# A graph layer on one core: the order of the work is set by a table of quarters, the taken edges run three quarters apart from iteration 36 on, extra tiles come every seven quarters, and two tiles are left behind the last sum

## The reference, cut to what matters

```
def reference(x, src, dst, edge_type_3, node_type_3, W_e, b_e, W_n, b_n):   # 6250 nodes, 106250 edges, D = 128
    parts = [relu(x)]
    for t in range(3):
        msg = relu(x[src] @ W_e[t].T + b_e[t])
        msg = where((edge_type == t)[:, None], msg, 0)
        parts.append(segment_sum(msg, dst, num_segments=6250))
    agg = concatenate(parts, axis=1)                       # 6250 x 512
    for t in range(3):
        updated = where((node_type == t)[:, None], agg @ W_n[t].T + b_n[t], updated)
    return layernorm(x + (updated + x), axis=-1)
```

## Time and profile before

| what | value |
|---|---|
| median of 3 runs | 921.31 us (919.78 to 922.39) |
| the profiled execution | 922.23 us, of which the span of instructions is 920.3 us |
| GpSimd's 630 indirect DMAs | 100.6 to 886.0 us |
| TensorE busy, VectorE busy, GpSimd busy | 80%, 63%, 73% of the span |

### The profile page before, as it was taken

The page is one execution under the profiler, slowest core; times in us unless marked ns, Lnnn a source line. Parts: engine busy times, 40 slices in busy tenths (PEclk is TensorE's granted clock), DMA queues, the critical chain, the costliest instruction groups (busy, mean ns, idle before and its releaser), DMA issues.

```text
span 920.3 us, 13773 instructions
## 1 busy us (share of the span) xinstructions
PE 738.3 (80%) x4555; PEld 602.0 (65%) x4555; DVE 584.0 (63%) x1429; ACT 183.2 (20%) x468; POOL 672.1 (73%) x718
## 2 busy tenths in 40 slices
PE   5593077998998888888988888888888888697796
PEld 3361066786877766776766776766776676576674
DVE  6999987367675565556555556556465555664755
ACT  3393011122111112112112112112111110110110
POOL 7777777777777777777777777777777777777740
PEclk9796578799999999999999999999999999998998
DMA  8594433334344234234234233333333443332311
GB/s 248 155 325 126 118 95 79 83 87 66 113 98 110 67 98 110 70 95 107 72 96 108 71 98 98 82 96 98 81 109 106 103 109 80 97 98 75 96 34 33
DMA packets 65779, 94.07 MB, mean 102 GB/s; under 512 B 16497, under 2 KB 49233, under 8 KB 65711
## 3 DMA queue, kind: packets, MB, share of 16 engines
q0 software_dynamic: 22432, 45.99, 20.8%
q1 hardware_dynamic: 40577, 43.14, 15.8%
q10 hardware_dynamic: 2702, 4.08, 1.6%
HBM read 80.23 MB, written 12.92 MB: 101 GB/s over the span
## 4 chain that ended last, share of the span: by engine, by line
POOL 36%; PE 27%; DVE 15%; issue 13%; DMA 7%; SPq 0%; DVEq 0%; ACT 0%
POOL tab L643 36%; PE ps L1556 7%; DMA tab<-message_table,idx_t 6%; PE ps L1573 6%; PE ps L1635 4%; PE ps L1543 2%; PE ps L1534 2%; PE ps L1596 2%; DVE src_wide L995 1%; DVE stage L1028 1%; PE ps L1587 1%; PE ps L1628 1%; DVE first_wide L931 1%; DMA dst_raw<-in_dst 1%; DVE dst_raw L988 1%
## 5 line engine op out<-in xcount | busy, mean ns | idle before, releaser
L643 POOL DMA_INDIRECT tab<-message_table,idx_t x630 | 594.7, 944 | 192.0 <-issue 185.0
L1556 PE MATMUL ps<-work,tab 128*128 128x126 f32 x1260 | 187.9, 292 | 114.2 <-DMA tab<-message_table,idx_t 90.1
L1149 DVE TENSOR_TENSOR work<-key_t,ps 128x378 f32<-128x378 f32 (+1 forms) x180 | 108.8, 606 | 262.2 <-PE ps L1556 256.4
L1556 PEld LDWEIGHTS ps<-work,tab 128*128 128x128 f32 x1260 | 166.0, 200 | 130.6 <-issue 73.8
L1165 DVE TENSOR_TENSOR acc<-ps,acc 128x126 f32 (+1 forms) x306 | 95.9, 314 | 29.0 <-DVE acc L1165 8.6
L1635 PE MATMUL ps<-wn_t,stage 128*128 128x384 f32 x288 | 100.7, 486 | 1.7 <-DVE stage L1289 1.7
L639 POOL DMA_INDIRECT xg<-in_x,esrc_t x67 | 71.4, 1066 | 20.8 <-issue 16.2
L1587 PE MATMUL ps<-we_t,order_f 128*128 128x128 f32 x540 | 84.1, 295 | 2.9 <-DVE acc L1165 2.9
L785 ACT ACTIVATE emsg<-ps 128x384 f32<-128x384 f32 x71 | 34.8, 490 | 254.5 <-PE ps L1535 254.5
L1587 PEld LDWEIGHTS ps<-we_t,order_f 128*128 128x128 f32 x540 | 73.0, 201 | 14.4 <-issue 11.3
L1635 PEld LDWEIGHTS ps<-wn_t,stage 128*128 128x128 f32 x288 | 54.6, 190 | 39.8 <-DVE stage L1289 1.9
(11 more groups left out here) (235 smaller groups left out, 875.3 us busy)
## 6 DMA issues: line engine op xcount, KB each, us to landing
tab<-message_table,idx_t POOLq DMA_INDIRECT x630, 2.5
message_table<-tab SPq DMA_DIRECT2D x24, 384.0 KB, 4.4
dst_raw<-dense_types SPq DMA_DIRECT2D x45, 192.0 KB
wn_raw<-message_table SPq DMA_DIRECT2D x22, 384.0 KB, 3.5
src_wide<-dense_lists SPq DMA_DIRECT2D x45, 128.0 KB, 3.4
xg<-in_x SPq DMA_DIRECT2D x11, 256.0 KB
work<-in_x ACTq DMA_DIRECT2D x10, 256.0 KB, 5.1
out<-xg SPq DMA_DIRECT2D x10, 256.0 KB
```

The source lines that it names most:

```text
L643: pool.indirect_dma_start(msg[:, slot, :], None, table, bass.IndirectOffsetOnAxis(ap=rows, axis=0)).then_inc(signal, 16)
L1149: dve.tensor_tensor(hot[:, first:first + n, :].rearrange("p c (t w) -> p c t w", w=WIN), keys.broadcast_to((P, n, T, WIN)), iota_win.rearr ...
L1556: ins = pe.matmul(sums_bank(j, g), msg[:, column, :], hot[:, column, :], start=(c == 0), stop=(c == n - 1))
```

## The change

The four copies of `iteration(j)` are replaced by `quarter(j, g)` on TensorE, VectorE and ScalarE, and every step is placed by a number of quarters behind a start (`dense_step`, `tile_step`, `EXTRAS`). Up to taken edges 36 the steps stand where they stood. From there on:

- The `dense_turn` of taken edges r stands in quarter `turn_at(r)`, which is 4 r + 3 up to r = 36 and then three quarters further for each r instead of four: 171, which is (42, 3), for r = 44. The mask comes 1 quarter later, make 3, sum 4 and add 5 quarters later, so the last add stands in quarter 176, (44, 0). For r above 36 `dense_add` reads its two row numbers with a `load_bases` of its own.
- SyncE's `load_dense_nodes` and `load_dense_types` follow that table.
- The extra tiles 48 to 45 start every 7 quarters from quarter 148 on, instead of every 8.
- A fourth staging buffer is laid over `work`. In the last iteration tile 41 goes through buffer 2, tile 42 through buffer 0, tile 43 through buffer 3 and tile 44 through buffer 1. Behind the last sum come the additions for tiles 43 and 44 as before, and now also the `finish_h` and `finish_y` of tile 42.
- The values of `added` come from one dictionary, `ADDED`, filled by `count_adds`.

```
+LEAD_FROM, LEAD_STEP = NE, 3
+def turn_at(r):
+    return NG * min(r, LEAD_FROM) + NG - 1 + LEAD_STEP * max(r - LEAD_FROM, 0)
+def pick_at(r):
+    return turn_at(r - 1) + 1 if r else NG // 2
+MASK_LATER, MAKE_LATER, SUM_LATER, ADD_LATER = 1, 3, 4, 5
+EXTRA_FROM, EXTRA_STEP = NG * (NE + 1), 7
+ACC_LATER, LINEAR_LATER, H_LATER, SD_LATER, Y_LATER = 2, 4, 5, 6, 7
...
             def iteration(j):
-                if j > 1:
-                    sp.wait_ge(d_made, j - 1)
-                    load_dense_types(j)
+                for r in range(2, NI):
+                    if j == (turn_at(r - 2) + MAKE_LATER) // NG + 1:
+                        sp.wait_ge(d_made, r - 1)
+                        load_dense_types(r)
...
+                r = dense_step(q, ADD_LATER)
+                if r is not None:
+                    dense_add(r, bases_of[NG:NG + SIDES] if r <= LEAD_FROM else load_bases(r + 2, NG, NG + SIDES))
...
             def last_iteration(j, bases_of):
                 dve.wait_ge(group_summed, NG * j + 1)
...
+                dense_add(j, load_bases(j + 2, NG, NG + SIDES))
+                for g in range(NG):
                     add_sums(j - 1, g, bases_of[g])
+                finish_acc(SPLIT, 0, 2, ADDED["main", j - 1, NG - 1])
...
                 dve.wait_ge(group_summed, NG * j + 4)
+                add_sums(j, 3, bases_of[3])
+                finish_acc(NA - 1, 0, 3, ALL_ADDS)
                 finish_acc(ORDER[KE], KE, 1, ALL_ADDS)
+                finish_h(SPLIT + 1, Z0_TILES - 1)
+                finish_h(NA - 1, 0, 3)
+                finish_y(SPLIT + 1, Z0_TILES - 1)
                 finish_h(ORDER[KE], KE, 1)
+                finish_y(NA - 1, 0, 3)
                 finish_y(ORDER[KE], KE, 1)
...
+            def last_iteration(j):
+                pe.wait_ge(stage_acc[0], SPLIT)
+                finish_turn(SPLIT, 0, len(BATCHES), 2, first=True)
+                pe.wait_ge(added, ADDED["main", j - 2, NG - 1])
                 sum_group(j, 0)
+                place_selfs(SPLIT, 0, 2)
+                finish_linear(SPLIT - 1)
                 sum_group(j, 1)
+                finish_linear(0, 2, first=True)
+                pe.wait_ge(stage_acc[2], 1)
+                finish_turn(SPLIT + 1, Z0_TILES - 1, len(BATCHES))
+                pe.wait_ge(added, ADDED["dense", j, SIDES - 1])
+                finish_turn(NA - 1, 0, len(BATCHES), 3, first=True)
                 pe.wait_ge(fin_var[1], KE)
                 finish_turn(ORDER[KE], KE, 2, 1)
+                pe.wait_ge(added, ADDED["main", j - 1, NG - 1])
+                sum_group(j, 2)
...
                 linear_open(KE, 1)
+                finish_linear(Z0_TILES - 1)
+                linear_open(0, 3, first=True)
+                pe.wait_ge(added, ADDED["main", j, 1])
                 sum_group(j, 3)
+                linear_types(0, 3)
                 linear_types(KE, 1)
```

More of the change, by code:

```diff
@@ L1344, in iteration @@
-                if extra and odd:
-                    finish_y(ORDER[nth], nth, 1)
+                if tile_step(q, Y_LATER) is not None:
+                    finish_y(tile_step(q, Y_LATER), tile_step(q, Y_LATER))
+                if q - Y_LATER in EXTRAS:
+                    finish_y(ORDER[EXTRAS[q - Y_LATER]], EXTRAS[q - Y_LATER], 1)
             def last_iteration(j, bases_of):
                 dve.wait_ge(group_summed, NG * j + 1)
-                dense_onehot(j)
-                dense_mask(j - 1)
@@ L1401, in _ @@
             for j in range(NI - 1):
-                iteration(j, bases_of)
+                for g in range(NG):
+                    quarter(j, g, bases_of)
                 if j == 0:
                     dve.wait_ge(acc_zeroed, 1 + 1 + 1 + 1 + 8 + 8)
-                bases_of = load_bases(j + 1, j < NE)
+                bases_of = load_bases(j + 1, 0, PLACES if j < NE else NG + SIDES if j < LEAD_FROM + 2 else NG)
                 if j == BAD_AT - 1:
@@ L1732, in _ @@
             for j in range(NI - 1):
-                iteration(j)
+                for g in range(NG):
+                    quarter(j, g)
             last_iteration(NI - 1)
```

417 lines of the change are left out of this document (186 added, 231 removed).

## The result

The changed kernel takes **912.63 us** (median of 4 runs, 911.22 to 913.44) where the kernel before takes 921.85 us on the same chip (919.78 to 926.08): a ratio of 0.988, 95% interval 0.986 to 0.991 (this is not the quotient of the medians, which is 0.990). The change made the kernel faster, but by 9.2 us instead of the 17.7 forecast, and 912.63 lies above the upper end of the range, 909.5.

What follows compares the result with a forecast made beforehand. GpSimd's gather issue bounds the middle; TensorE, 19 us late, sets the end. 18.7 us saved less 1.0 lost is 17.7; 921.31 (0.9 below the profiled execution) less 17.7 gives 903.6 us, own range 901 to 906, 8 in 10 up to 909.5.

Steps and rivals of the forecast that it cites:

- What bounds the middle: From 100.6 to 887 us GpSimd issues gathers without waiting, 1.249 us each, 17.48 us per iteration of 14.
- the 10.2 us of tolerance: Buffers let a group sum come at least 10.2 us late before GpSimd waits; beyond that each us is lost.
- Part 1: Iterations 37 to 43, taken edges three quarters apart: TensorE's 14.8 us of work fit in 17.48, cost nothing.
- The place that the walk had named as the worst: Behind (39, 3): extra linear, make of 39 and turn of 40, 7.0 us in a row, next sum some 5 us late.
- shorter chain waits for itself: Rival: TensorE waits for VectorE, losing 2 to 3 us at each of seven taken-edge sets; 904 to 909; chance 0.12.
- waits and clock as two rivals: Waits: the shorter chain, 904 to 909, chance 0.12. Clock: last iteration at low clock, 906.6 to 909.6, chance 0.17.
- VectorE's reads of row numbers: Iterations 37 to 43: new reads cost 0 to 1.5 us per iteration, taken as 0.7, hidden behind VectorE's group waits.
- SyncE's loads at nothing: Loads of types come four quarters ahead of their mask, three for the last ones, 13 us; costed at nothing.
- Part 2: Last iteration: TensorE waits for (44, 1), VectorE's last addition begins at 891.0 instead of 909.66; 18.7 us saved.
- The 2.65 us for landing: Time from the start of a group's last gather until TensorE can take up its data.
- Part 3: One more tile behind the last sum: last addition to last `finish_y` 8.85 us instead of 7.84; 1.0 us lost.
- The pressed iterations: Rival, iterations 37 to 43: low TensorE clock loses 10.5 us per iteration and delays gathers; 935 us; chance 0.03.

Runs made afterwards that it cites:

- the run with filled waits: Changed kernel plus idle TensorE products, 15 in quarter 160 and 20 ahead of the make of taken edges 43: 909.80 us, ratio 0.986 to the kernel before.
- the second trace: Trace of the changed kernel run once more with no edit: 910.54 us, ratio 0.986 to the kernel before.
- the even chain: Changed kernel, beyond taken edges 36 turn one quarter later and make, sum, add 2, 3, 4 quarters behind it: 906.39 us, ratio 0.982; again 906.34, 0.982.

## Why the prediction was wrong, step by step

**What bounds the middle: right.** Gathers at 1.249 us with gaps of 0.30 issue from start to end, and the 10.2 us of tolerance were well found. The two groups that made GpSimd wait at the end were 11.3 us late ((43, 0): landed 858.2, summed 869.48) and 10.8 us ((43, 1): its last gather started at 860.54, so landed 863.2, summed 873.96), and it lost 0.28 and 0.73 us. The tolerance of 10.2 us is that of a group of four chunks; one of three, like (43, 0), has one gather more, some 11.4. The first gap, 0.15 us, came behind (40, 1), 9.9 us late.

**Part 1, TensorE's iterations 37 to 43 at nothing: the step that failed.** The work itself was costed well: 4.2 us for make and turn are 4.27 in the run with filled waits. But the walk of its list knew only TensorE's own work and the data. It took VectorE as hidden "behind its group waits". In fact VectorE is released only once per quarter, by a group sum. When TensorE has 7 us in one quarter and 1 us in the next two, VectorE idles first and then is the one that TensorE waits for. At (42, 3) this was 4.58 us of wait, and 3.7 more for the clock behind it (2.5 in the second trace). (44, 1) was then summed 7.9 us after the forecast 879.93. Not all of that comes from this place. Between (43, 0) and (44, 1) stands the second wait for VectorE, 1.47 us at 883.16, which the forecast hadn't either; TensorE's own work there is 16.9 us. So with neither, TensorE would have come to (44, 1) at 878.1, ahead of its data. By this estimate 6.4 of the 7.9 us are the wait and the clock at (42, 3), and 1.5 are the second wait. From the sum of (43, 0) the list ran through: the last addition came 29.3 to 29.5 us behind it in all six traces with the changed kernel's order, whether (43, 0) was summed at 865.70 or at 874.14.

The place that the walk had named as the worst, behind (39, 3), shows the same mechanism. The next sum was to be some 5 us late there, and it was 10.6 (816.17, last gather at 802.88):

```profile
807.45 0.34 PE L1638 MATMUL ps<-bn_parts,pick_parts 128*128 128x384 bf16 x1 [3.74 <-DVE stage L1330]
```

The 3.74 us are a wait for VectorE, and the linear's six passes behind it took 3.59 us and not 1.94. It cost the end nothing, since at (42, 3) TensorE had caught up to 1.4 us.

So the "shorter chain waits for itself" was the case that came, with a chance of only 0.12. Its place was right (make needs the additions made one quarter earlier), and its price too small: I let the wait cost 2 to 3 us of slack per set of taken edges and entry into iteration 44 up to 5 us late, and not the clock on top. I had priced waits and clock as two rivals, 904 to 909 and 906.6 to 909.6, and neither range holds 912.6. In these traces the one brought the other, and the 3.7 us of clock on top of 909 would reach it.

The Trainium skill ("TensorE: Matmul & The Clock Gate", What's actually happening) has the throttled state as the default, released by activity. I used it against the end of the kernel only, and there it did not come: from 870.38 to 898.80 the granted clock was 1.00. By that rule the make behind a wait of 4.58 us is where to look, and the trace agrees: 7.99 us for 4.27.

**VectorE's reads of row numbers**, 0.7 us per iteration: too much. In the changed kernel the additions of taken edges 42 start at 860.34, where the one-hot ahead of them just ends (859.83 and 0.54 make 860.37), and for five more of the eight sets from 37 on the gap is 0.07 us or less. For taken edges 40 there is one:

```profile
834.48 0.90 DVE L1207 TENSOR_TENSOR acc<-ps,acc 128x216 f32 x2 [0.67 <-issue]
```

For taken edges 44 the addition starts at 885.68, 0.77 us behind the end of the sum that releases VectorE (884.91), where the one-hot at 853.90 starts 0.05 us behind its own. So two reads can cost some 0.7 us, but they did it in two of eight places, and the 0.7 were charged to every iteration. Why there and not elsewhere no run tells.

**SyncE's loads at nothing: right.** No wait of TensorE or VectorE in iterations 37 to 43 ends with them.

**Part 2: right as a walk, wrong in its start.** From the sum of (44, 1) to the last addition I had 879.93 to 891.0, 11.1 us. The changed kernel took 887.82 to 898.97, 11.15; the even chain 881.65 to 892.88, 11.23. What failed is the condition that stood ahead of it, that TensorE would be waiting for (44, 1). With the even chain it was (0.81 us of wait for the data). The 2.65 us for landing held there (881.65, last gather at 879.02), but it was read from one row and is the short end. In the trace before, the wait of TensorE for the data of (43, 3) ended 3.90 us after the group's last gather (TensorE, then GpSimd):

```profile
872.45 2.05 PE L1556 MATMUL ps<-work,tab 128*128 128x126 f32 x8 [3.49 <-DMA tab<-message_table,idx_t]
```

```profile
868.55 0.94 POOL L643 DMA_INDIRECT tab<-message_table,idx_t  x1 [0.30 <-issue]
```

Such waits from (36, 3) on ended 2.62 to 4.09 us after the last gather. So each lateness given here may be up to 1.4 us too large; what makes the difference stays open.

**Part 3, 1.0 us: right.** The tail took 8.56 us (898.97 to 907.53), forecast 8.85, before 7.84: 0.7 us lost. That the additional `finish_h` fills VectorE's wait of 1.70 us in the earlier trace rows was shown by moving it away: the wait came back, and the tail only fell to 8.29. The end behind the last `finish_y` grew from 2.8 to 3.4 us, here and in the even chain. I had it as unchanged, and no run tells why.

**The sum** for the span: 8.0 us for the last addition, less 0.3 for the tail, plus 0.6 behind it make 8.3, and the span was 910.9 instead of 902.6. The rest of the miss, 0.8 of the 9.0 us between 912.63 and 903.6, is the last term: the median was to lie 0.9 us below the profiled execution, and it lay 0.1 below (912.74).

**The pressed iterations**, as a slower case, did not come. In the run with 4.3 us more at (42, 1) one sees how near they were: there GpSimd lost 4.04 and 0.72 us at once. A slip in that rival changes nothing: 14.8 us of work at half the clock are 29.6 and not "some 28", so an iteration would lose 12.1 us and not 10.5.

## What to carry to other kernels

Two engines that release each other once per stage can come near the sum of their stages' maxima, not the maximum of their sums. So a walk of one engine's list isn't enough where steps are moved closer together: walk both, release by release, and look for the stage in which one has all its work and the other none. Place steps of a chain so that two heavy ones never share a stage; here the same instructions, moved by a quarter, gave 4 us. And price a wait of TensorE of some microseconds in front of much work together with the slow clock behind it: in these traces 2.5 to 3.7 us on 4.3 us of work, though the medians have not shown that taking the low clock away alone gives it back.

## What the runs showed of the hardware

- A wait of about the same length is not always followed by the low clock. 1.00 and 0.95 us in the two traces of the even chain: the next six passes 0.94 us. 0.93 us in the kernel with `finish_h` moved: 1.23, then 1.65, and (43, 1) summed 2.8 us later in all. 2.08 us ahead of the sum of taken edges 44 in the even chain's first trace: 0.97 us for four passes; 1.83 us at the same place in its second: 1.78. 1.67 us of wait for data at 853.97 in that trace: full speed.
- Ahead of the make of 43, behind waits of 3.08 to 8.87 us, the low clock came each time (five traces), and behind 2.55 and 1.13 us with one group sum between them as well, unless products filled the wait. How long it lasted differed: make and turn took 6.7 to 8.0 us, also in two traces of one program with the same wait.
- Idle products in a wait of 4.6 us brought full speed for what followed (4.27 us instead of 6.7 to 8.0), for no gain in the median that could be told.
- The buffers' tolerance is a sharp edge: at 10.8 us late GpSimd lost 0.73 us, and with 4.3 us more work ahead of the wait it lost 4.04 and 0.72.
- An indirect gather's data were waited for until 2.62 to 4.09 us after the start of the group's last gather (the kernel before, from (36, 3) on).
